# Four layer norms: inverse square root by a power on Pool with one Newton step, for a bit seed with three

## The chip, the cores and the metric

The kernel runs on one NeuronCore of one Trainium2 chip. The metric is the device time of one execution in microseconds (us): the median over several executions. A core has five engines that run their own instruction streams in order: PE (TensorE, matrix products; PEld is its weight load), DVE (VectorE), ACT (ScalarE), POOL (GpSimd) and SP (SyncE, which only issues transfers here). They wait for each other through semaphores, and an engine that waits holds everything queued behind.

## The reference

The input is x of 16 sequences (b) by 256 tokens by 128 features, float32. Two transformer-like layers follow, each a sum of a residual and a block on a layer norm:

```python
def _layernorm(x, axis=-1, eps=1e-05):
    m = jnp.mean(x, axis=axis, keepdims=True)
    v = jnp.var(x, axis=axis, keepdims=True)
    return (x - m) / jnp.sqrt(v + eps)

x = x + softmax_attention(_layernorm(x), ...)     # 16 heads of 8, scores 256 x 256
x = x + recurrence(_layernorm(x), ...)            # state over the 16 sequences: c = f*c + i*g; h = tanh(x wo + c uo + bo)
x = x + linear_attention(_layernorm(x), ...)      # rope, elu + 1 features, kv = sum k v, out / denom
x = x + mixture_of_experts(_layernorm(x), ...)    # 16 experts, the best 2 of each token, gelu between two products
```

So four norms are taken of every token. One norm needs 1/sqrt(v + eps) for each token. Tokens lie on the 128 partitions, two tiles of 128 tokens to a sequence (`TT = 2`), so the inverse roots of a sequence and a norm are a 128x2 array: very little data, and a chain of dependent steps.

## The kernel before

The program has three stages, each a block in which every engine runs its own loop over n, and each engine's instructions are written out by hand in a fixed order. Sequence b is at a different point of the pipeline in each part: "lag k" below is work on sequence n-k in iteration n.

**Stage 1** (`attention_and_recurrence`, n from -2 to 20) has softmax attention and the recurrence. PE does scores twice (once in p_max for the row maxima, which DVE reduces in `row_max`, L396, and once in p_exp, which ACT exponentiates, L551). Norm 1 of sequence n+2 and norm 2 of sequence n-3 run in iteration n. For each, DVE takes mean and variance in `layer_stats` (bn_stats, bn_aggr into `mv`), then three small instructions make the seed: v = var + eps (L382), the bits of v shifted right by one (L384), and 0x5F3759DF minus that (L387). Pool then does `newton_steps` (L67 to L74, four instructions a step, three steps) on the 128x2 array, and `layer_norm` (L315, L317: subtract the mean, multiply by the root). Behind each norm of sequence n+2 Pool has `setup` (once) and the split of q and k into bfloat16 parts (L337, L340, L342), which SP writes to a scratch array in DRAM and reads back as QS and KS before PE can start the scores.

**Stage 2** (`linear_attention_and_routing`, n from 0 to 20) has the h of the recurrence, linear attention, norms 3 and 4, and the routing to experts. Norm 3 of sequence n and norm 4 of sequence n-3 share one 128x4 array `root[r]`. Before the change DVE does the whole root in `root_step`, 13 instructions (L1012, L1015, L1019, then three times L1027, L1029, L1031, then L1035, which makes -mean*root), put one by one between DVE's other instructions. Signals `sd` and `nw` count them. ACT waits for `nw` before xn3 of sequence n-1 (L1267) in iteration n, and before `pay`, norm 4 of n-4 (L1302). ACT runs in this order in an iteration: xn3 (lag 1), hT = tanh(zs) (lag 0, L1273), on3T, xn3T, the exp and relu of rot, pay (lag 4), and more. PE, also in order, turns on3 (lag 3), xn3 (lag 1) and hT (lag 0; all L1349), then does p_u (L1376) and p_qkv (L1385, L1387). DVE adds p_h and p_u into X (L1078, L1085), casts the places of the tokens of sequence n-5 into `pos` (L1090), takes the statistics, makes rope products t (L1138 to L1149), KVm (L1167), the routing (among them z, L1202, and wheref, L1213), and ends with zs of the next iteration (L1054).

Pool in stage 2 has, per iteration: four indirect DMAs that scatter the rows of sequence n-5 into `disp` (L969, they wait for `pos`), an update of the row numbers (L976), the residual add of sequence n-4 (L983), and rot of sequence n-1, the sum of two rope products (L990).

**Stage 3** (`experts`) runs 80 tiles of 128 tokens through their experts, gathers and adds; the change doesn't touch it.

`steady` is an empty instruction that stops two instructions from being joined.

Of the kernel before, what the change touches and what calls it, by code (L numbers as in the profile page):

```python
# [13 lines left out]
P = 128  # L14
# [16 lines left out]
MAGIC = 0x5F3759DF  # L31
NEWTON = 3
# [27 lines left out]
def newton_steps(t, pool, root, mark, b):  # L60

    y, u, v = root[:, 0, :], root[:, 1, :], root[:, 3, :]
    j = 0
    for _ in range(NEWTON):
        if j:
            pool.wait_ge(mark.sem, mark.at(b, j))
        pool.tensor_tensor(u, y, y, ALU.mult).then_inc(mark.sem, 1)  # L67
        pool.wait_ge(mark.sem, mark.at(b, j + 1))
        pool.tensor_tensor(u, u, v, ALU.mult).then_inc(mark.sem, 1)
        pool.wait_ge(mark.sem, mark.at(b, j + 2))  # L70
        steady(pool, t)
        pool.tensor_scalar(u, u, -0.5, 1.5, ALU.mult, ALU.add).then_inc(mark.sem, 1)
        pool.wait_ge(mark.sem, mark.at(b, j + 3))
        pool.tensor_tensor(y, y, u, ALU.mult).then_inc(mark.sem, 1)  # L74
        j += 4


def constants(pool, t, w):

    n = 0  # L80
    fills = [(t["ident"], 0.0), (t["ident16"], 0.0), (w["kv_mask"], 1.0), (w["before"], 1.0),
# [29 lines left out]
def attention_and_recurrence(nc, ctx, t, out_dbg=None):  # L111
# [8 lines left out]
    with ExitStack() as scope:  # L120
# [57 lines left out]
        seed_a = sig("seed_a", 3)  # L178
        newton_a = sig("newton_a", 4 * NEWTON)
# [29 lines left out]
        seed_b = sig("seed_b", 3)  # L209
        newton_b = sig("newton_b", 4 * NEWTON)  # L210
# [87 lines left out]
        def _(pool):  # L298
# [20 lines left out]
            newton = lambda root, mark, b: newton_steps(t, pool, root, mark, b)  # L319

            def iteration(n, r):
                if active(n, -2):
                    pool.wait_ge(seed_a.sem, seed_a.at(n + 2))
                    q = (r + 2) % RING
                    newton(root1[q], newton_a, n + 2)
                    if xnT_p.due(n + 2 - RING):
                        pool.wait_ge(xnT_p.sem, xnT_p.at(n + 2 - RING))
                    layer_norm(n + 2, mv1[q], root1[q], xn1[q], newton_a, norm_a)
# [23 lines left out]
                if active(n, 3):  # L352
                    b, q = n - 3, (r - 3) % RING
                    pool.wait_ge(seed_b.sem, seed_b.at(b))
                    newton(root2[q], newton_b, b)
                    if xn2T_p.due(b - RING):
                        pool.wait_ge(xn2T_p.sem, xn2T_p.at(b - RING))
                    layer_norm(b, mv2[q], root2[q], xn2[q], newton_b, norm_b)
# [4 lines left out]
        def _(dve):  # L363
# [7 lines left out]
            def layer_stats(b, stats, mv, root, st, sd, prev_norm):  # L371
# [5 lines left out]
                for i in range(TT):  # L377
# [3 lines left out]
                dve.wait_ge(st.sem, st.at(b))  # L381
                dve.tensor_scalar(root[:, 3, :], mv[:, :, 1], EPS, None, ALU.add).then_inc(sd.sem, 1)  # L382
                dve.wait_ge(sd.sem, sd.at(b, 1))
                dve.tensor_scalar(root[:, 4, :].bitcast(U32), root[:, 3, :].bitcast(U32), 1, None, ALU.logical_shift_right)\  # L384
                    .then_inc(sd.sem, 1)
                dve.wait_ge(sd.sem, sd.at(b, 2))
                dve.tensor_scalar(root[:, 0, :].bitcast(I32), root[:, 4, :].bitcast(I32), -1.0, float(MAGIC), ALU.mult, ALU.add)\  # L387
                    .then_inc(sd.sem, 1)
# [50 lines left out]
            def iteration(n, r):  # L439
# [8 lines left out]
                for s in range(8):  # L448
# [26 lines left out]
                    if s == 5 and active(n, 3):  # L475
                        b, q = n - 3, (r - 3) % RING
                        dve.wait_ge(x1_s.sem, x1_s.at(b))
                        layer_stats(b, stats2[q], mv2[q], root2[q], stats_b, seed_b, norm_b)
# [4 lines left out]
                    if s == 1 and active(n, -2):  # L483
                        q = (r + 2) % RING
                        layer_stats(n + 2, stats1[q], mv1[q], root1[q], stats_a, seed_a, norm_a)
# [279 lines left out]
def linear_attention_and_routing(nc, ctx, t):  # L765
# [5 lines left out]
    with ExitStack() as scope:  # L771
# [46 lines left out]
        st3, sd, nw, nm3 = sig("st3", 4), sig("sd", 3), sig("nw", 3 * NEWTON + 1), sig("nm3", 2)  # L818
# [109 lines left out]
        def _(pool):  # L928
# [25 lines left out]
            def iteration(n, r):  # L954
# [23 lines left out]
                if active(n, 4):  # L978
# [5 lines left out]
                        .then_inc(res.sem, 1)  # L984
                if active(n, 1):
# [9 lines left out]
        def _(dve):  # L995
            def root_step(m, r, step):

                if not (active(m, 0) or active(m, 3)):
                    return
                y, u, shift, v = (root[r][:, j, :] for j in range(4))  # L1000
                newton = step - 3
                if step == 0:

                    if active(m, 0):
                        dve.wait_ge(st3.sem, st3.at(m))
                    if active(m, 3):
                        dve.wait_ge(st4.sem, st4.at(m - 3))
                    if active(m, PAIR):
                        dve.wait_ge(nm3.sem, nm3.at(m - PAIR))
                    if nm4.due(m - 3 - PAIR):  # L1010
                        dve.wait_ge(nm4.sem, nm4.at(m - 3 - PAIR))
                    dve.tensor_scalar(v, mv[r][:, :, 1], EPS, None, ALU.add).then_inc(sd.sem, 1)  # L1012
                elif step == 1:
                    dve.wait_ge(sd.sem, sd.at(m, 1))
                    dve.tensor_scalar(u.bitcast(U32), v.bitcast(U32), 1, None, ALU.logical_shift_right).then_inc(sd.sem, 1)  # L1015
                elif step == 2:

                    dve.wait_ge(sd.sem, sd.at(m, 2))
                    dve.tensor_scalar(y.bitcast(I32), u.bitcast(I32), -1.0, float(MAGIC), ALU.mult, ALU.add).then_inc(sd.sem, 1)  # L1019
# [724 lines left out]
```

## Time and profile before

| what | us |
|---|---|
| median of 3 runs | 832.79 (830.95 to 838.27) |
| the profiled execution, its own time | 830.77 |
| its span in the profile | 828.8 |
| busy: PE / DVE / POOL / ACT | 607.7 / 508.8 / 365.4 / 343.1 |
| stage 1, stage 2, stage 3 (about) | 0 to 405, 405 to 641, 641 to 829 |
| mean granted TensorE clock | 0.88 of full speed |

The time of the profiled execution is 2.0 us more than the span, which goes from the first to the last instruction. Busy times are sums of one engine's instructions and say nothing about who waits for whom; the rows further down do. The stages meet at barriers, so a time saved within a stage moves everything behind it.

### The profile page before, as it was taken

To read this page: it belongs to the slowest core of one execution; us is meant where nothing else is said; L and a number is where in the kernel's file an instruction comes from. 1 tells how busy PE (TensorE), PEld (TensorE's weight loads), DVE (VectorE), ACT (ScalarE), POOL (GpSimd) and SP (SyncE) were. 2 spreads that over 40 slices of the span, in tenths; PEclk is the share of its full clock that TensorE was granted. 3 is DMA by queue.
4 is the path that set the end of the run, shared out by engine and by line. 5 is a ranking of instruction groups with operands and counts; after the bars stand their busy time and mean duration, and the time that the engine had idled before them with its cause. 6 is when DMAs were issued, how large, how long until landed. Compare 5 with 4: busy or idle time off the path is not lost. (4 is left out here: it accounts for less than half of the span.)

```text
span 828.8 us, 17046 instructions
## 1 busy us (share of the span) xinstructions
PE 607.7 (73%) x4308; PEld 412.5 (50%) x4309; DVE 508.8 (61%) x1745; ACT 343.1 (41%) x725; POOL 365.4 (44%) x747
## 2 busy tenths in 40 slices
PE   1378899999999999997457667667662388788850
PEld 0134555555555555554235455445442277677740
DVE  6277877777777777753177887888765122222214
ACT  1015666666666666663224444444431122222210
POOL 5533555555555553222311345455446055555553
PEclk9999999999999999998666787787655599999995
DMA  5333332222222222100430000000001322222108
GB/s 139 95 109 96 99 98 82 79 73 76 79 72 73 77 78 76 34 2 1 80 129 2 16 24 27 13 26 23 20 23 50 78 76 72 72 71 74 53 15 302
DMA packets 49537, 55.62 MB, mean 67 GB/s; under 512 B 11229, under 2 KB 42658, under 8 KB 46914
## 3 DMA queue, kind: packets, MB, share of 16 engines
q1 hardware_dynamic: 43714, 45.87, 19.5%
q0 software_dynamic: 4608, 8.47, 3.1%
q8 instruction: 28, 0.46, 0.2%
q10 hardware_dynamic: 1152, 0.53, 0.2%
q14 instruction: 35, 0.29, 0.1%
HBM read 36.44 MB, written 19.02 MB: 67 GB/s over the span
## 5 line engine op out<-in xcount | busy, mean ns | idle before, releaser
L396 DVE TENSOR_REDUCE negmax<-p_max 128x2 f32<-128x512 f32 x256 | 172.6, 687 | 63.9 <-PE p_max L605 63.0
L551 ACT ACTIVATE probs<-p_exp 128x1024 f32<-128x1024 f32 x128 | 129.3, 1025 | 9.4 <-PE p_exp L580 9.4
L1536 POOL DMA_INDIRECT back<-y,rows x80 | 78.3, 979 | 84.1 <-DVE y L1597 61.0
L605 PE MATMUL p_max<-KS,QS 96*128 96x256 bf16 x512 | 102.4, 286 | 9.3 <-DMA QS<-scratch 6.9
L969 POOL DMA_INDIRECT disp<-pay,pos x64 | 63.0, 984 | 94.9 <-ACT pay L1302 49.7
L67 POOL TENSOR_TENSOR root<-root 128x2 f32<-128x2 f32 x96 | 18.6, 193 | 170.1 <-DVE root L387 165.0
L595 PE MATMUL p_out<-probs,V 128*32 128x256 f32 x1024 | 81.8, 391 | 1.3 <-ACT OT L567 0.7
L580 PE MATMUL p_exp<-QS,KS 128*128 128x256 bf16 x512 | 78.0, 275 | 2.5 <-DMA QS<-maxT 2.5
L1597 DVE TENSOR_TENSOR y<-p_y,rows 128x256 f32<-128x256 f32 x40 | 16.9, 424 | 100.1 <-PE p_y L1661 88.2
L605 PEld LDWEIGHTS p_max<-KS,QS 96*128 96x128 bf16 x512 | 43.6, 100 | 55.2 <-DVE negmax L396 25.5
L1648 PE MATMUL p_hid<-xT,w 128*128 128x128 f32 x320 | 59.5, 307 | 0.0
L580 PEld LDWEIGHTS p_exp<-QS,KS 128*128 128x128 bf16 x512 | 48.1, 98 | 18.0 <-issue 7.8
L1616 ACT ACTIVATE hid<-p_hid 128x512 f32<-128x512 f32 x40 | 23.9, 598 | 75.7 <-remote 49.2
L1661 PE MATMUL p_y<-W,hid 128*128 x320 | 51.0, 294 | 0.0
L1648 PEld LDWEIGHTS p_hid<-xT,w 128*128 128x128 f32 x320 | 49.8, 196 | 1.5
L1646 PE MATMUL p_hid<-ones,bp 128*128 128x128 bf16 x160 | 35.8, 224 | 14.6 <-issue 13.5
L1661 PEld LDWEIGHTS p_y<-W,hid 128*128 128x128 f32 x320 | 41.8, 190 | 1.9
L1611 ACT ACTIVATE xT<-p_x 128x256 f32<-128x256 f32 x40 | 15.3, 381 | 49.3 <-PE p_x L1634 46.9
L1590 DVE COPY w<-W 128x256 f32 x80 | 22.7, 303 | 19.0 <-issue 19.0
L595 PEld LDWEIGHTS p_out<-probs,V 128*32 128x32 f32 x1024 | 20.2, 108 | 27.5 <-issue 19.9
L1439 PE MATMUL p_r<-sel,before 128*128 128x16 bf16 x16 | 3.1, 191 | 40.7 <-DVE sel L1242 40.7
L990 POOL TENSOR_TENSOR rot<-t 128x512 f32<-128x512 f32 x16 | 20.2, 1262 | 27.8 <-DVE t L1149 27.8
(229 smaller groups left out, 1367.6 us busy)
## 6 DMA issues: line engine op xcount, KB each, us to landing
KS<-scratch SPq DMA_DIRECT2D x16, 576.0 KB
QS<-scratch SPq DMA_DIRECT2D x48, 192.0 KB
scratch<-part SPq DMA_DIRECT2D x16, 384.0 KB, 2.7
rows<-disp SPq DMA_DIRECT2D x80, 65.0 KB
yb<-back SPq DMA_DIRECT2D x8, 512.0 KB, 6.5
W<-in_W_dram SPq DMA_DIRECT2D x1, 2064.0 KB, 8.8
W<-in_W_dram SPq DMA_DIRECT2D x1, 2048.0 KB, 13.1
out_dram<-X SPq DMA_DIRECT2D x8, 256.0 KB, 5.9
```

Of the source, the lines that this page charges most:

```text
L396: dve.tensor_reduce(negmax[:, i, 2 * hp:2 * hp + 2], p_max[u % 2][:, :].rearrange("p (h k) -> p h k", h=2), AX.X, ALU.max, negate=True).th ...
L551: act.activation(probs[s % 2][:, :, :].rearrange("p j q -> p (j q)"), p_exp[s % 2][:, :], ACT.Exp)\
L580: mm = pe.matmul(p_exp[s % 2][:, j * S:(j + 1) * S], KS[q][:, h, kt * P:(kt + 1) * P], QS[q][:, h, :], start=True, stop=True)
L595: mm = pe.matmul(p_out[32 * j:32 * j + 32, 0:S], V[q][:, kt, 4 * g + j, :], probs[s % 2][:, j, :], start=(kt == 0), stop=(kt == 1))
L605: mm = pe.matmul(p_max[u % 2][:, j * S:(j + 1) * S], QS[q][0:PADDED, h, i * P:(i + 1) * P], KS[q][0:PADDED, h, :], start=True, stop=True)
L969: pool.indirect_dma_start(out=disp, out_offset=bass.IndirectOffsetOnAxis(ap=pos[o][:, i, k:k + 1], axis=0), in_=pay[o][:, k, i, :], in_off ...
L1536: pool.indirect_dma_start(out=back, out_offset=bass.IndirectOffsetOnAxis(ap=rows[r][:, h, D + 1:ROW].bitcast(U32), axis=0), in_=y[r][:, h, :],
L1590: dve.tensor_copy(w1[r][:, h, :], w["W1"][:, bass.ds(es[h], 1), 0:HID].rearrange("p o c -> p (o c)")).then_inc(w_s.sem, 1)
L1616: act.activation(hid[q][:, :, :, :].rearrange("p h c t -> p (h c t)"), p_hid[q % 2][:, :], ACT.Gelu).then_inc(hid_s.sem, 1)
L1646: pe.matmul(dst, w["bp"][:, bass.ds(es[h], 1), c * P:(c + 1) * P].rearrange("p o c -> p (o c)"), w["ones16"][:, :], start=True, stop=False)
L1648: mm = pe.matmul(dst, w1[q][:, h, c * P:(c + 1) * P], xT[q][:, h * P:(h + 1) * P], start=False, stop=True)
L1661: mm = pe.matmul(dst, hid[q][:, h, c, :], w["W2"][:, bass.ds(es[h], 1), c, :].rearrange("p o c -> p (o c)"), start=False, stop=(c == 1))
```

## The change

Pool's newton_steps becomes `inverse_root`: v = var + eps, then y = v to the power -0.5 as a tensor_tensor operation with an array `power` that holds -0.5, then one Newton step of four instructions. The seed instructions leave DVE in stage 1. In stage 2 all of `root_step` leaves DVE; Pool does inverse_root on the 128x4 array and two more instructions for -mean*root, eight in all, between the residual add (L983) and rot (L990). `nw` now counts eight, and DVE's and ACT's waits for `nw` stay where they were. One memset, of `power`, is added to `constants`.

```diff
-MAGIC = 0x5F3759DF
-NEWTON = 3
+ROOT_STEPS = 6
...
-def newton_steps(t, pool, root, mark, b):
+def inverse_root(t, pool, var, root, mark, b):
     y, u, v = root[:, 0, :], root[:, 1, :], root[:, 3, :]
...
+    steady(pool, t)
+    pool.tensor_scalar(v, var, EPS, None, ALU.add).then_inc(mark.sem, 1)
+    pool.wait_ge(mark.sem, mark.at(b, 1))
+    pool.tensor_tensor(y, v, t["power"][:, 0:v.shape[1]], ALU.pow).then_inc(mark.sem, 1)
+    pool.wait_ge(mark.sem, mark.at(b, 2))
+    pool.tensor_tensor(u, y, y, ALU.mult).then_inc(mark.sem, 1)
+    pool.wait_ge(mark.sem, mark.at(b, 3))
+    pool.tensor_tensor(u, u, v, ALU.mult).then_inc(mark.sem, 1)
+    pool.wait_ge(mark.sem, mark.at(b, 4))
+    steady(pool, t)
+    pool.tensor_scalar(u, u, -0.5, 1.5, ALU.mult, ALU.add).then_inc(mark.sem, 1)
+    pool.wait_ge(mark.sem, mark.at(b, 5))
+    pool.tensor_tensor(y, y, u, ALU.mult).then_inc(mark.sem, 1)
...
# stage 1, Pool, norm 1 (norm 2 alike)
-                    pool.wait_ge(seed_a.sem, seed_a.at(n + 2))
+                    pool.wait_ge(stats_a.sem, stats_a.at(n + 2))
-                    newton(root1[q], newton_a, n + 2)
+                    inverse_root(t, pool, mv1[q][:, :, 1], root1[q], root_a, n + 2)
...
# stage 1, DVE, layer_stats
-                dve.tensor_scalar(root[:, 3, :], mv[:, :, 1], EPS, None, ALU.add).then_inc(sd.sem, 1)
-                dve.tensor_scalar(root[:, 4, :].bitcast(U32), root[:, 3, :].bitcast(U32), 1, None, ALU.logical_shift_right)\
-                dve.tensor_scalar(root[:, 0, :].bitcast(I32), root[:, 4, :].bitcast(I32), -1.0, float(MAGIC), ALU.mult, ALU.add)\
...
# stage 2, Pool, between the residual add and rot; root_step and its 13 calls leave DVE
+                if active(n, 0) or active(n, 3):
+                    if active(n, 0):
+                        pool.wait_ge(st3.sem, st3.at(n))
+                    if active(n, 3):
+                        pool.wait_ge(st4.sem, st4.at(n - 3))
...
+                    inverse_root(t, pool, mv[r][:, :, 1], root[r], nw, n)
+                    pool.wait_ge(nw.sem, nw.at(n, ROOT_STEPS))
+                    pool.tensor_tensor(root[r][:, 2, :], mv[r][:, :, 0], root[r][:, 0, :], ALU.mult).then_inc(nw.sem, 1)
+                    pool.wait_ge(nw.sem, nw.at(n, ROOT_STEPS + 1))
+                    steady(pool, t)
+                    pool.tensor_scalar(root[r][:, 2, :], root[r][:, 2, :], -1.0, None, ALU.mult).then_inc(nw.sem, 1)
```

Where the instructions stand in the program can be seen at two places.

On Pool in stage 2, in an iteration of the steady part (here the first behind the hardware loop), before:

```order
L969 DMA disp<-pay,pos 67712x130 x4
L976 TENSOR_SCALAR pay<-pay 128x4
L983 TENSOR_TENSOR X<-X,pay 128x256
L990 TENSOR_TENSOR rot<-t 128x512
L969 DMA disp<-pay,pos 67712x130 x4
```

and the same iteration now:

```order
L956 DMA disp<-pay,pos 67712x130 x4
L963 TENSOR_SCALAR pay<-pay 128x4
L970 TENSOR_TENSOR X<-X,pay 128x256
L63 TENSOR_SCALAR root<-mv 128x4
L65 TENSOR_TENSOR root<-root,power 128x4
L67 TENSOR_TENSOR root<-root 128x4
L69 TENSOR_TENSOR root<-root 128x4
L72 TENSOR_SCALAR root<-root 128x4
L74 TENSOR_TENSOR root<-root 128x4
L986 TENSOR_TENSOR root<-mv,root 128x4
L989 TENSOR_SCALAR root<-root 128x4
L995 TENSOR_TENSOR rot<-t 128x512
```

The eight root instructions stand behind the four DMAs and the residual add, and rot behind them.

On DVE in stage 2, from the last statistics of an iteration on, before:

```order
L1116 BN_AGGR mv<-stats_1 128x2 x2
L1012 TENSOR_SCALAR root<-mv 128x4
L1126 SCALAR_TENSOR_TENSOR feat<-ex,rl 128x512
L1015 TENSOR_SCALAR root<-root 128x4
L1019 TENSOR_SCALAR root<-root 128x4
L1027 TENSOR_TENSOR root<-root 128x4
L1138 TENSOR_TENSOR t<-p_qkv,cosf 128x512
L1029 SCALAR_TENSOR_TENSOR root<-root 128x4
L1143 TENSOR_TENSOR t<-p_qkv,sinf 128x64x4
L1031 SCALAR_TENSOR_TENSOR root<-root 128x4
L1149 TENSOR_TENSOR t<-p_qkv,sinf 128x64x4
L1027 TENSOR_TENSOR root<-root 128x4
```

and now:

```order
L1098 TENSOR_TENSOR t<-p_qkv,cosf 128x512
L1102 TENSOR_TENSOR t<-p_qkv,sinf 128x64x4
L1107 TENSOR_TENSOR t<-p_qkv,sinf 128x64x4
L1115 TENSOR_REDUCE negtop<-p_r 128x2
L1123 TENSOR_TENSOR KVm<-p_kvo,kv_mask 128x144
```

The 13 root instructions are gone, and the others keep their order.

## Rows read from the trace of the kernel before

**Rows 1.** The page: span, and busy time of each engine.

```profile
span 828.8 us, 17046 instructions
PE 607.7 (73%) x4308; PEld 412.5 (50%) x4309; DVE 508.8 (61%) x1745; ACT 343.1 (41%) x725; POOL 365.4 (44%) x747
```

**Rows 2.** Who waited for whom, 100 to 400 us: total, times, longest.

```profile
POOL root L67 <- DVE root L387: 122.6, 25, 13.9
PE p_misc L693 <- DVE maxpart L411: 11.6, 13, 1.3
```

**Rows 3.** Timeline of POOL, the first 25 us: start, duration, instruction.

```profile
10.38 0.19 POOL L67 TENSOR_TENSOR root<-root 128x2 f32<-128x2 f32 x1 [6.32 <-DVE root L387]
10.65 0.20 POOL L69 TENSOR_TENSOR root<-root 128x2 f32<-128x2 f32 x1
11.01 0.19 POOL L72 TENSOR_SCALAR root<-root 128x2 f32<-128x2 f32 x1 [0.17 <-POOL root L69]
...
13.97 0.61 POOL L315 TENSOR_TENSOR xn<-X,mv 128x256 f32<-128x256 f32 x1
...
17.89 0.19 POOL L67 TENSOR_TENSOR root<-root 128x2 f32<-128x2 f32 x1
...
22.87 1.15 POOL L337 TENSOR_TENSOR rest<-qk,part 128x512 f32<-128x512 f32 x1
```

**Rows 4.** Timeline of DVE, and then of PE, in the same start of stage 1.

```profile
9.24 0.37 DVE L380 BATCH_NORM_AGGREGATE mv<-stats 128x2 f32<-128x6 f32 x2
...
38.68 1.04 PE L605 MATMUL p_max<-KS,QS 96*128 96x256 bf16 x4 [6.92 <-DMA QS<-scratch]
```

**Rows 5.** Timeline of DVE in stage 2, one steady iteration from pos to pos.

```profile
536.14 0.16 DVE L1090 CAST pos<-posf 128x4 uint32<-128x4 f32 x1
...
537.27 0.25 DVE L1116 BATCH_NORM_AGGREGATE mv<-stats 128x2 f32<-128x6 f32 x2
...
540.94 0.31 DVE L1167 TENSOR_TENSOR KVm<-p_kvo,kv_mask 128x144 f32<-128x144 f32 x1 [0.26 <-PE p_kvo L1413]
...
543.37 1.21 DVE L1213 CAST wheref<-where 128x4 f32<-128x4 uint32 x1
...
545.59 0.42 DVE L1054 TENSOR_TENSOR zs<-p_h,UC 128x256 f32<-128x256 f32 x1
...
548.56 0.16 DVE L1090 CAST pos<-posf 128x4 uint32<-128x4 f32 x1
```

**Rows 6.** Timeline of POOL in the same iteration.

```profile
537.43 1.06 POOL L969 DMA_INDIRECT disp<-pay,pos  x1 [5.93 <-ACT pay L1302]
...
542.65 0.68 POOL L983 TENSOR_TENSOR X<-X,pay 128x256 f32 x1
543.29 1.26 POOL L990 TENSOR_TENSOR rot<-t 128x512 f32<-128x512 f32 x1
```

**Rows 7.** Timeline of DVE: pos of iterations 6 and 15.

```profile
473.40 0.16 DVE L1090 CAST pos<-posf 128x4 uint32<-128x4 f32 x1
...
585.94 0.16 DVE L1090 CAST pos<-posf 128x4 uint32<-128x4 f32 x1
```

**Rows 8.** From xn3 to PE's turn of hT: ACT and PE timelines, iteration 2.

```profile
426.31 0.88 ACT L1267 ACTIVATE xn<-X,root 128x128 f32<-128x128 f32 x2 [1.91 <-DVE root L1035]
...
427.73 0.63 PE L1349 MATMUL p_h<-ident,hT 128*128 128x128 f32 x2
```

**Rows 9.** Chain of work that ended last: PE's turn of hT, iteration of rows 5.

```profile
546.78 0.43 PE p_h L1349 x2
```

**Rows 10.** Timeline of DVE: X gets p_h in iterations 1 and 2, before any scatter.

```profile
419.87 0.42 DVE L1078 TENSOR_TENSOR X<-p_h,X 128x256 f32<-128x256 f32 x1 [1.78 <-PE p_h L1349]
...
428.40 0.42 DVE L1078 TENSOR_TENSOR X<-p_h,X 128x256 f32<-128x256 f32 x1 [1.78 <-PE p_h L1349]
```

**Rows 11.** End of stage 2, iteration 18: residual add on POOL, and pay on ACT.

```profile
627.54 0.68 POOL L983 TENSOR_TENSOR X<-X,pay 128x256 f32<-128x256 f32 x1
...
628.67 1.09 ACT L1302 ACTIVATE pay<-X,root 128x256 f32<-128x256 f32 x2 [3.68 <-issue]
```

More of the change, by code:

```diff
@@ L57, in steady @@
     eng.nop(nofuse=True)
-def newton_steps(t, pool, root, mark, b):
+def inverse_root(t, pool, var, root, mark, b):
     y, u, v = root[:, 0, :], root[:, 1, :], root[:, 3, :]
[L63 to L75, printed above, removed]
+    steady(pool, t)
[11 more added lines that the diff above has]
+    pool.tensor_tensor(y, y, u, ALU.mult).then_inc(mark.sem, 1)
 def constants(pool, t, w):
     n = 0
-    fills = [(t["ident"], 0.0), (t["ident16"], 0.0), (w["kv_mask"], 1.0), (w["before"], 1.0),
+    fills = [(t["power"], -0.5), (t["ident"], 0.0), (t["ident16"], 0.0), (w["kv_mask"], 1.0), (w["before"], 1.0),
              (w["ones16"], 1.0), (w["one_row"], 1.0)]
@@ L369, in _, with layer_stats @@
             dve.wait_ge(t["v_set"].sem, 6)
-            def layer_stats(b, stats, mv, root, st, sd, prev_norm):
+            def layer_stats(b, stats, mv, st, prev_norm):
                 steady(dve, t)
@@ L984, in iteration @@
                         .then_inc(res.sem, 1)
+                if active(n, 0) or active(n, 3):
[3 more added lines that the diff above has]
+                        pool.wait_ge(st4.sem, st4.at(n - 3))
+                    if at(n, 0):
+                        pool.wait_ge(mv_set.sem, PAIR)
+                    if active(n, PAIR):
+                        pool.wait_ge(nm3.sem, nm3.at(n - PAIR))
+                    if nm4.due(n - 3 - PAIR):
+                        pool.wait_ge(nm4.sem, nm4.at(n - 3 - PAIR))
+                    inverse_root(t, pool, mv[r][:, :, 1], root[r], nw, n)
[4 more added lines that the diff above has]
+                    pool.tensor_scalar(root[r][:, 2, :], root[r][:, 2, :], -1.0, None, ALU.mult).then_inc(nw.sem, 1)
                 if active(n, 1):
@@ L995, in _ @@
         def _(dve):
[L996 to L1019, printed above, removed]
-                elif newton < 3 * NEWTON:
-                    if newton:
-                        dve.wait_ge(nw.sem, nw.at(m, newton))
-                    else:
-                        dve.wait_ge(sd.sem, sd.at(m))
-                    if newton % 3 == 0:
-                        dve.tensor_tensor(u, y, y, ALU.mult).then_inc(nw.sem, 1)
-                    elif newton % 3 == 1:
-                        dve.scalar_tensor_tensor(out=u, in0=u, scalar=-0.5, in1=v, op0=ALU.mult, op1=ALU.mult).then_inc(nw.sem, 1)
-                    else:
-                        dve.scalar_tensor_tensor(out=y, in0=u, scalar=1.5, in1=y, op0=ALU.add, op1=ALU.mult).then_inc(nw.sem, 1)
-                else:
-                    dve.wait_ge(nw.sem, nw.at(m, 3 * NEWTON))
-                    dve.scalar_tensor_tensor(out=shift, in0=mv[r][:, :, 0], scalar=-1.0, in1=y, op0=ALU.mult, op1=ALU.mult).then_inc(nw.sem, 1)
             def wide(ap, shape):
@@ L1678, in program @@
         t["back"] = nc.dram_tensor("back", [TOP * TOKENS, D], F32).ap()
-        t["count"] = sb("count", [P, E])
+        t["count"], t["power"] = sb("count", [P, E]), sb("power", [P, 2 * TT])
         w = t["w2"] = dict(wo=sb("wo", [P, D]), uo=sb("uo", [P, D]), bo=sb("bo2", [P, 1]), Wqkv2=sb("Wqkv2", [P, 3 * D]),
```

39 lines of the change are left out of this document (9 added, 30 removed).

## The prediction

> **What bounds the kernel now.** I read the page's engine line first, then the table of waits of stage 1, then the timelines of Pool, DVE, ACT and PE where a root is made. The page shows PE and DVE ahead of Pool in busy time [rows 1], which seems to say that work should go from DVE to Pool. The other views say where this is so.
>
> In the steady part of stage 1 it isn't worth anything. Pool stood idle for 122.6 us in 300 before it got a seed, 25 times [rows 2], so its norms are nowhere late, and PE runs through; its largest wait for DVE is 11.6 us in all for the split of the maxima [rows 2], which starts behind the last row maximum and not behind a seed. Only the start of stage 1 hangs on roots: Pool is the path there. It starts the first root at 10.38, the first norm at 13.97, the second root at 17.89, and can split q and k of the first sequence only at 22.87 [rows 3]; PE's first scores at 38.68 wait for the transfers that follow from it [rows 4].
>
> In stage 2 the busy DVE is not the engine that sets the pace. Follow one iteration from pos to pos, 536.14 to 548.56, 12.42 us [rows 5]. The cast gives pos; Pool's four scatters start at 537.43, the residual add at 542.65, rot at 543.29, and rot ends at 544.55 [rows 6]. DVE's cast of 4 columns to wheref starts at 543.37 and takes 1.21 us, so it ends when rot does [rows 5]. From its end DVE runs through to zs and to the next pos in 4.0 us. So the loop goes through Pool: pos, scatters, add, rot, wheref, pos. Over nine iterations the mean is (585.94 - 473.40)/9 = 12.50 us [rows 7]. KVm in the middle waits for PE [rows 5], so DVE's first half wouldn't be much earlier without root instructions either.
>
> The Trainium skill (SBUF — State Buffer, section "SBUF: two separate sides") says that an operation of GpSimd and one of VectorE with two SBUF inputs or in a two-port mode lock each other out for a whole instruction. The wheref row agrees. By that rule each of eight new Pool instructions could hold a DVE instruction of this kind once; at 0.2 us each this would be 1.6 us of DVE's time an iteration, against the 1.2 us that the wait of wheref gives back.
>
> **The power.** No row shows one. I call its excess e the time that it takes beyond the 0.19 us of a multiply of the same shape [rows 3]. From below it is zero, as it can't be done faster than a multiply. From above the nearest row is a scatter, in which Pool works through 128 descriptors in 1.06 us [rows 6]: e up to 0.9. I take e = 0.3 for 128x4 and half of that for 128x2, nearer to the multiply, since 4 columns are little for 128 lanes; this is a guess between the two, and the largest open cost. A dearer power is a rival below.
>
> **Part by part.** Steps of a chain on Pool start 0.27 us apart, and 0.36 us where `steady` stands between [rows 3].
>
> Start of stage 1. The statistics end at 9.61 [rows 4]; the first norm may start at 9.66 + 0.27 (v) + 0.27 (power) + 0.27 + 0.36 + 0.27 + 0.34 = 11.44 + e/2, for 13.97 now [rows 3]: -2.5 (0.7 of it are DVE's three seed instructions). The second root has six instructions for twelve: 1.85 for 3.7, another -1.9. Together -4.4 + e = **-4.1 us**; it all comes through, as Pool is without a gap from there to the split, but for a set-up that moves along. The added memset is one of 0.2 us at the head, beside six us of idle Pool ahead of the first root: nothing.
>
> Steady part and end of stage 1: **0**. Covered by the idle Pool time; if the cover were gone, the 2 x 6 instructions fewer would be a gain of 3 us an iteration, so it is no risk either. DVE's six seed instructions, under 1.4 us an iteration (twice the 0.7 above), stand beside a PE that doesn't wait for them.
>
> Stage 2, first iterations. There are no scatters yet, and a root on Pool starts right behind the statistics. Its chain is eight steps: 0.28 + 0.28 + 0.28 + 0.37 + 0.28 + 0.28 + 0.37 and 0.23 for the last = 2.4 to 2.5 + e (a hundredth each for 4 columns in place of 2). From X to X iterations 1 and 2 are 8.53 us apart [rows 10]. Now: X to the end of statistics 1.36 (pos to the end of statistics is 1.38 in rows 5, and here X stands in the place of pos), 0.06, root 2.45 + e, then from the start of xn3 to PE's turn of hT 1.42 [rows 8] and 0.67 to X [rows 8, 10]: 6.0 + e, a gain of 2.5 - e. The next three intervals have more DVE work of their own, and gain what 13 small instructions (0.16 us for the cast of 4 columns, [rows 5], so 2.1 together) leave beside waits for PE: bounds are 0 and 2.1 each, and I take 1.1, 1.1 and 0.5, the last with less since Pool's add comes in. In iteration 0 Pool may still be busy with the split of the biases (see the program); I estimate the root there late by 0.3 + e, for which no row is shown. Sum: -4.9 + 2e = **-4.3 us**.
>
> Stage 2, steady. In front of xn3 (ACT), and so in front of hT behind it, and PE's turn of xn3 and hT, now stands Pool's root, which stands behind four scatters. From rows 5, 6: pos to first scatter 1.29, first scatter to the end of the add 5.86, root 2.45 + e, xn3 to the turn of hT 1.42 [rows 8], the turn of hT at 546.78 [rows 9] to the next pos at 548.56, 1.78. Sum 12.80 + e, against 12.50 now: +0.3 + e. Rot is later by 2.45 + e too, but the wait for it by wheref is gone, since wheref now comes ahead of rot; DVE by itself would need about 11.4 us (12.5 less the 1.0 by which wheref is longer than a cast of 4 columns, 0.16, [rows 5]), which is covered by the new path. Eleven intervals, from iteration 5 to 16, hold a norm 3 in this place: 11 x 0.6 = **+6.6 us**. With e from 0 to 0.9 and the first term from -0.3 to +0.5 (the 1.29 is 1.0 in other iterations, where the new path has less to fill): 0 to +15.
>
> Stage 2, end. The root of iteration 18 was ready early. Now it follows the add, which ends at about 628.2 [rows 11], and takes to 630.7 + e; pay, which started at 628.67 [rows 11], can start only then: +2.1 + e; the last scatters and the plan of the tiles follow from it, and a few tenths from the wait of iteration 16's pay. **+2.7 us**.
>
> Sum: -4.1 - 4.3 + 6.6 + 2.7 = +0.9, so the profiled execution's 830.8 becomes 831.7. The median of the three runs is 2.0 above that execution, so I forecast 833 as a median.
>
> **Rivals.**
> Slow power: if Pool evaluates it element after element, e is above 1. It decides from e = 0.8 on (e stands in the sum 1 + 2 + 11 + 1 = 15 times, so each 0.1 costs 1.5 us). At e = 2 the sum is -4.4 - 4.9 + 3.3 + 2.4 + 15 x 2 = +26, 859 us. For it: nothing else on Pool in the trace is a transcendental, and its other work is cheap only because it is a multiply or an add. Against: one remaining Newton step fits a fast, rough evaluation. This is the case on the slower side.
>
> DVE is the bound after all: Pool's root comes early enough, or the clock of PE rises as the pace does, and each steady interval loses the wait of wheref or the 13 instructions, about 1.1 us. Then -4.1 - 4.3 - 12 + 2.7 = -18, 815 us. For it: DVE is busy in most of stage 2. Against: the order on Pool puts the root behind 7.2 us of other work.
>
> The first power waits for code: a routine is loaded when Pool meets the instruction first, in the start of stage 1, on the path. The trace shows no such gap for Pool's first instruction of other kinds [rows 3]. By bounds between nothing and the 4.1 us that this part gains, the sum would be up to 4 higher, 837.
> The Trainium skill (GPSIMD Engine Reference, section "Instruction dispatch") says about 6 us for the first call of a freshly loaded kernel; the sum would be 839 by it. No row shows one.
>
> The change may also not do what it says in one way: if the compiler turned the power into several instructions; that is the slow power again.
>
> **How the numbers follow.** 1% (8 us) is about what a measurement of this kernel can tell from no change. Forecast (e up to 0.8): 0.57, 825 to 841. Slow power: 0.24, 841 to 870 or more. DVE bound: 0.15, 812 to 824. Code load: 0.04, near 838. Faster by over 1%: 0.15 and 0.03 of the forecast's low edge = 0.18. Slower by over 1%: 0.24 and 0.11 of its high edge and of the code load = 0.35. The rest, 0.47, is within 1%. The range from 820 to 858 leaves out a tenth at either side.
>
> **What the profile after would show.** The power's row on Pool gives e. The first norm at about 11.6 for 13.97, PE's first scores at about 34.6. In stage 2 wheref at 0.2 us instead of 1.2, ACT's xn3 waiting for Pool's last root instruction, hT right behind xn3, pos to pos near 13.1. If pos to pos falls below 12, the Pool path isn't what I take it for; if it is over 14, the power is slow or Pool's small instructions are held by DVE.

## The result, and the profile after

The changed kernel takes 840.88 us (median, 837.61 to 844.65), the kernel before 832.22 us (829.03 to 838.27) on the same chip: a ratio of 1.009, 95% interval 1.007 to 1.011 (the quotient of the two medians is 1.010, within that interval). It is 0.9% slower, where I had forecast +0.1%.

The page of the changed kernel, with the group of the new instruction (columns as in [rows 1]; in the group: instructions, busy time and mean ns of one, idle time before them):

```profile
span 837.3 us, 16537 instructions
...
PE 607.3 (73%) x4308; PEld 413.0 (49%) x4309; DVE 449.9 (54%) x1402; ACT 341.9 (41%) x725; POOL 395.6 (47%) x708
...
L65 POOL TENSOR_TENSOR root<-root,power 128x2 f32<-128x2 f32 (+1 forms) x51 | 42.8, 839 | 4.2
```

DVE lost 58.9 us of busy time [rows 1], Pool gained 30.2, and the span grew by 8.5. The power alone is 42.8 us of Pool's time.

The start of stage 1, Pool and then PE:

```profile
9.77 0.24 POOL L63 TENSOR_SCALAR root<-mv 128x2 f32<-128x2 f32 x1 [5.66 <-DVE mv L375]
10.10 0.72 POOL L65 TENSOR_TENSOR root<-root,power 128x2 f32<-128x2 f32 x1
...
12.14 0.61 POOL L312 TENSOR_TENSOR xn<-X,mv 128x256 f32<-128x256 f32 x1
...
16.17 0.22 POOL L63 TENSOR_SCALAR root<-mv 128x2 f32<-128x2 f32 x1
...
19.77 1.16 POOL L332 TENSOR_TENSOR rest<-qk,part 128x512 f32<-128x512 f32 x1
...
35.14 1.03 PE L592 MATMUL p_max<-KS,QS 96*128 96x256 bf16 x4 [6.49 <-DMA QS<-scratch]
```

The first norm starts at 12.14 for 13.97 [rows 3], the split at 19.77 for 22.87, PE's first scores at 35.14 for 38.68 [rows 4]: -3.5 us. The very first power takes 0.72 us, as the later ones of two columns do, so no load shows in it.

One steady iteration of stage 2, from pos to pos, on DVE:

```profile
531.56 0.16 DVE L1054 CAST pos<-posf 128x4 uint32<-128x4 f32 x1
...
536.45 0.31 DVE L1123 TENSOR_TENSOR KVm<-p_kvo,kv_mask 128x144 f32<-128x144 f32 x1 [0.49 <-issue]
...
538.21 0.61 DVE L1164 CAST wheref<-where 128x4 f32<-128x4 uint32 x1
...
539.82 0.42 DVE L1018 TENSOR_TENSOR zs<-p_h,UC 128x256 f32<-128x256 f32 x1
...
540.72 0.22 DVE L1038 TENSOR_REDUCE posf<-mine 128x4 f32<-128x64 f32 x1
544.44 0.42 DVE L1042 TENSOR_TENSOR X<-p_h,X 128x256 f32 x1 [3.49 <-PE p_h L1300]
...
545.63 0.16 DVE L1054 CAST pos<-posf 128x4 uint32<-128x4 f32 x1
```

and on Pool:

```profile
532.84 1.10 POOL L956 DMA_INDIRECT disp<-pay,pos  x1 [3.93 <-ACT pay L1253]
...
538.11 0.68 POOL L970 TENSOR_TENSOR X<-X,pay 128x256 f32 x1
538.88 0.22 POOL L63 TENSOR_SCALAR root<-mv 128x4 f32<-128x4 f32 x1
539.18 1.04 POOL L65 TENSOR_TENSOR root<-root,power 128x4 f32<-128x4 f32 x1
...
541.85 0.24 POOL L989 TENSOR_SCALAR root<-root 128x4 f32<-128x4 f32 x1 [0.16 <-POOL root L986]
542.05 1.26 POOL L995 TENSOR_TENSOR rot<-t 128x512 f32<-128x512 f32 x1
```

and what waits for the root on ACT, then PE's turn of hT:

```profile
542.23 0.49 ACT L1218 ACTIVATE xn<-X,root 128x128 f32 x1 [4.98 <-POOL root L989]
...
543.64 0.63 PE L1300 MATMUL p_h<-ident,hT 128*128 128x128 f32 x2
```

DVE is done with everything it has at 540.94, and then stands idle for 3.49 us. It waits for PE. There p_h waits for hT, hT stands behind xn3 in ACT's order, and xn3 waits 4.98 us for Pool's last root instruction. The root itself starts when the four scatters and the residual add are issued, though its input, mv, is ready at 532.94. That is the path of the prediction. It is 14.07 us long, by its five pieces: pos to first scatter 1.28, first scatter to root 6.04, root to xn3 3.35, xn3 to the turn of hT 1.41, on to pos 1.99. The two pos that answer to [rows 7]:

```profile
460.86 0.16 DVE L1054 CAST pos<-posf 128x4 uint32<-128x4 f32 x1
...
587.51 0.16 DVE L1054 CAST pos<-posf 128x4 uint32<-128x4 f32 x1
```

(587.51 - 460.86)/9 = 14.07 us, for 12.50. At the end of the stage pay waits 6.63 us for the last root, where it had waited for no root before [rows 11], and starts at 636.23, for 628.67:

```profile
636.23 1.09 ACT L1253 ACTIVATE pay<-X,root 128x256 f32<-128x256 f32 x2 [6.63 <-POOL root L989]
```

Set side by side at the same events, the 8.5 us of the span are: first scores -3.5; on to the first X of stage 2 another -4.6; from there to the pos of iteration 5 -4.6; iterations 5 to 16 +15.4; 16 to 20 +4.7; from there to the first transpose of stage 3 -0.7; stage 3 +1.7.

### The profile page after: what moved, and what is told of

Read it like the earlier page. It is cut to its first block, busy times and chain, and to the rows that moved or that the text cites. A ratio compares the mean times of both kernels' runs of the same rounds, so it can differ in the third digit from the quotient of the medians.

```text
span 837.3 us, 16537 instructions
## 1 busy us (share of the span) xinstructions
PE 607.3 (73%) x4308; PEld 413.0 (49%) x4309; DVE 449.9 (54%) x1402; ACT 341.9 (41%) x725; POOL 395.6 (47%) x708
## 4 chain that ended last, share of the span: by engine, by line
PE 19%; POOL 11%; issue 10%; ACT 4%; DVE 3%; DMA 2%; SPq 1%; POOLq 1%; another core or an unknown queue 0%; ACTq 0%; DVEq 0%
PE p_hid L1599 5%; PE p_y L1612 5%; POOL disp L956 5%; POOL root L65 2%; PE p_hid L1597 2%; PE p_ta L1300 1%; ACT pay L1253 1%; PE p_x L1585 1%; POOL X L970 1%; PE p_y L1609 1%; ACT xn L1218 1%; DMA yb<-back 1%; ACT rl L1243 1%; PE p_u L1327 1%; DVE X L1476 1%
## 5 line engine op out<-in xcount | busy, mean ns | idle before, releaser
L63 POOL TENSOR_SCALAR root<-mv 128x2 f32<-128x2 f32 (+1 forms) x51 | 12.2, 240 | 207.4 <-DVE mv L375 195.5
L567 PEld LDWEIGHTS p_exp<-QS,KS 128*128 128x128 bf16 x512 | 48.3, 98 | 19.4 <-issue 7.8
L65 POOL TENSOR_TENSOR root<-root,power 128x2 f32<-128x2 f32 (+1 forms) x51 | 42.8, 839 | 4.2
L1612 PEld LDWEIGHTS p_y<-W,hid 128*128 128x128 f32 x320 | 41.9, 190 | 2.5 <-issue 0.5
L1218 ACT ACTIVATE xn<-X,root 128x128 f32<-128x128 f32 (+1 forms) x32 | 14.0, 485 | 61.8 <-POOL root L989 61.8
L1300 PE MATMUL p_ta<-ident,xn 128*128 128x128 f32 x32 | 10.6, 432 | 33.1 <-ACT xn L1218 33.1
```

What stands on the lines that cost most here:

```text
L65: pool.tensor_tensor(y, v, t["power"][:, 0:v.shape[1]], ALU.pow).then_inc(mark.sem, 1)
L567: mm = pe.matmul(p_exp[s % 2][:, j * S:(j + 1) * S], KS[q][:, h, kt * P:(kt + 1) * P], QS[q][:, h, :], start=True, stop=True)
L1612: mm = pe.matmul(dst, hid[q][:, h, c, :], w["W2"][:, bass.ds(es[h], 1), c, :].rearrange("p o c -> p (o c)"), start=False, stop=(c == 1))
```

## The experiments

Chips differ (the kernel before took 833.7, 837.5 and 822.1 us beside the three groups of four runs), so ratios to it are compared, and intervals inside a trace. "Interval" is (pos of iteration 16 less pos of iteration 5)/11: 12.53 us before, 13.94 after. The first and the last of these eleven can be short or long by themselves, so where it matters the mean of the nine between iterations 6 and 15 is given too: 12.50 before, 14.07 after.

**The change in one stage only.** First stage 1 alone:

```diff
 # stage 1
-newton(root1[q], newton_a, n + 2)
+inverse_root(t, pool, mv1[q][:, :, 1], root1[q], root_a, n + 2)
 # stage 2: root_step on DVE as before
```

> The change in stage 1 alone; stage 2 keeps its 13 root instructions on DVE. By the two traces stage 1 of the changed kernel ends 8.1 us earlier (last state 404.34 and 396.24), in three places: the start, the last two iterations, and 0.17 us in each steady iteration. If these belong to the change, this kernel takes 832.2 - 8.1 = 824 us, a ratio of 0.990. If only the start does, as I forecast, and the rest is chance between two executions, it is 832.2 - 3.5 = 828.7, 0.996.

825.2 us, ratio 0.991 (0.987 to 0.995). Then stage 2 alone, with the bit seed left in stage 1:

> The change in stage 2 alone; stage 1 keeps the bit seed and three Newton steps. By the traces stage 2 loses 15.4 us from iteration 5 to 16 and about 5 at its end, and gains 4.5 in its first iterations: 832.2 + 16.7 = 849 us, ratio 1.020. The sum of the prediction with the measured power (e = 0.85) gives +12.7 + 3.2 - 3.2 = +12.7, 845, ratio 1.015. A rival by which DVE was the bound and stage 2 gained has it at or under 832.

850.1 us, ratio 1.019 (1.015 to 1.023), interval 14.06. So the change is two changes of opposite sign: about -8 us in stage 1 and +16 in stage 2. Both runs came out where the two traces had put them; of the two forecasts for stage 1 alone, the one by which only the start gains (0.996) lies outside the measured interval.

**The power as a multiply.** The same instructions, with a cheap one in the power's place (the roots are then not roots):

```diff
-    pool.tensor_tensor(y, v, power, ALU.pow)
+    pool.tensor_tensor(y, v, power, ALU.mult)     # power filled with 0.3
```

> The changed kernel with a multiply in the place of the power on Pool (by 0.3, so that the roots are wrong, and with them what follows), all else the same. It takes 0.84 us less on 128x4 and 0.53 less on 128x2. If the root lies on the path where I think, it is 11 x 0.84 in the steady part of stage 2, 3 x 0.84 at its ends and 2 x 0.53 at the start, with two more of 0.53 at the end of stage 1: 840.9 - 13.9 = 827 us, 0.994 of the kernel before. If Pool is not the path in stage 2, only the ends gain: 837 us or more.

830.3 us, ratio 0.995 (0.992 to 0.997), as expected. The interval is 13.29 us: of the 1.41 us by which it grew, 0.65 go with the power's excess (I had expected all of its 0.84), and 0.76 would be there with a power as cheap as a multiply.

**The root ahead of the scatters.** Pool's order in stage 2: root, scatters, row numbers, residual add, rot.

```diff
+                # root of iteration n, first on Pool
                 if active(n, 5):
                     # four scatters
                 ...
-                # root of iteration n
                 # rot
```

> The changed kernel with Pool's eight root instructions of stage 2 ahead of the four scatters in place of behind the residual add; the same instructions. The root starts at the statistics (1.4 us after pos) and xn3 waits no more; scatters, add and rot come 3.3 us later, rot at about 11 us after pos, which holds exp, relu and pay of the next iteration. I estimate 12.0 to 12.4 us from pos to pos in place of 14.0: 840.9 - 18 to 22 - 3 (end of stage 2) = 817 to 820 us, ratio 0.983. If the loss comes from the amount of work on Pool or from its hold on DVE, not from the place of the root, it stays at 838 or above.

837.95 us, ratio 1.006 (1.003 to 1.008): only 3 us of the 20 that I expected, and the very time that I had given the rival, more work on Pool. The interval is 13.51 us (14.13 between iterations 6 and 15), short and long ones in turn: 9.2, 18.3, 10.0, 18.5 and so on. Pool, DVE and ACT of this kernel, around a pos:

```profile
543.44 1.26 POOL L995 TENSOR_TENSOR rot<-t 128x512 f32<-128x512 f32 x1
543.75 0.98 DVE L1054 CAST pos<-posf 128x4 uint32<-128x4 f32 x1
...
544.73 0.63 ACT L1242 ACTIVATE ex<-rot 128x512 f32<-128x512 f32 x1 [3.15 <-POOL rot L995]
...
545.27 0.61 ACT L1243 ACTIVATE rl<-rot 128x512 f32<-128x512 f32 x1
...
545.79 1.08 ACT L1253 ACTIVATE pay<-X,root 128x256 f32 x2
```

The root no longer waits; rot does. It is now last on Pool, and ACT's order is ex, rl, pay, so pay, on which the router depends, waits for rot too, though it doesn't use it. Whether that is the cause, or the amount of work on Pool, the next run has to tell.

**Root and rot ahead of the scatters.**

> The changed kernel, with Pool's order in stage 2 turned to root, rot, then scatters, row numbers, residual add. With the root alone ahead (the run before this one) every second interval was long: rot stood last, ACT's ex, rl and with them pay waited for it. Theory, rot's place held that version back: pay no longer waits 3 us for rot, the interval from pos to pos falls from 14.1 to some 12.2 us, and the time is 820 us, ratio 0.985. Rival, Pool itself is full (root 3.3, rot 1.3, scatters 5, add 1.3, together 10.9 us, and what DVE locks out): the interval stays over 13 us and the time is 833 or more.

828.07 us, ratio 0.990 (0.985 to 0.996), interval (588.55 - 450.82)/11 = 12.52, between the theory and the rival. The work on Pool is the same as in the changed kernel, so the loss there came from its order: the places of root and rot together are worth 1.4 us an iteration, or 1.0 by the nine inner ones (13.03 for 14.07). By these this kernel is still 0.5 slower an iteration than the one before, and it gains only what it gets ahead of the first scatters: 41.1 us from the first X to the pos of iteration 5, for 46.4. I had expected 12.2. ACT's pay now waits for the scatters, whose buffer it fills:

```profile
528.12 1.09 ACT L1253 ACTIVATE pay<-X,root 128x256 f32 x2 [2.12 <-DMA disp<-pay,pos]
```

The trace shows another wait too, which the scatters and the add on Pool bring with them. Pool's residual add, and DVE's add of p_u just ahead of pos:

```profile
526.72 0.68 POOL L994 TENSOR_TENSOR X<-X,pay 128x256 f32 x1
...
527.50 0.42 DVE L1049 TENSOR_TENSOR X<-p_u,X 128x256 f32 x1 [1.92 <-PE p_u L1327]
```

Nothing in the program makes DVE's add wait for Pool's. Yet in the six iterations from 488 to 554 us it starts 0 to 0.15 us after Pool's ends. Pool has no gap to speak of from the root on: from pos at 514.97 to the root 1.6 us, then root, rot, scatters and add up to 527.40, then pos at 527.84. So in this order Pool's own work is the loop, which is what the rival said, if at a smaller price.

**Only rot ahead, the root still last.** The fourth corner of the square:

> The changed kernel with only rot moved ahead of the scatters, the root still last. Theory, the path is pos, statistics, t, rot, scatters, add, root, xn3, hT, pos: rot starts some 4 us behind pos in place of a scatter at 1.3, everything behind it is later by about 4 us, interval 18 us, time 880 or more. Rival, moving rot forward is what helped the other version, and the root's place matters little: 14 us or less an interval, 838 or less.

884.89 us, ratio 1.075 (1.071 to 1.079), interval 17.76. Pool in one iteration:

```profile
547.52 0.24 POOL L995 TENSOR_SCALAR root<-root 128x4 f32<-128x4 f32 x1 [0.16 <-POOL root L992]
554.84 1.26 POOL L948 TENSOR_TENSOR rot<-t 128x512 f32<-128x512 f32 x1 [7.07 <-DVE t L1107]
```

Pool stands idle for 7.07 us, because its first instruction waits for t, and the scatters, for which pos is there at 551.30, stand behind it. Of the four orders, ratios 1.009 (both last), 1.006 (root first), 1.075 (rot first), 0.990 (both first), only the last is faster than the kernel before. It is no faster than the change in stage 1 alone (0.991), so no order shows a gain from the root's move to Pool in stage 2.

**The power in the good order.** Root and rot first, and the power a multiply as above:

> The changed kernel with root and rot ahead of the scatters (0.990), and the power replaced by a multiply by a constant, so that the roots are not roots and the routing differs. Theory, in this order the root is off the path in the steady part: interval 12.4 to 12.5 us as with the power, and only the start and the first iterations gain, 3 to 5 us, ratio 0.985. Rival, the power still stands on the path: 11 times 0.85 more, ratio 0.974.

802.42 us, ratio 0.976 (0.972 to 0.979), interval (579.81 - 449.31)/11 = 11.86. I expected no change of interval; it fell by 0.66 us (by 1.1 between iterations 6 and 15, from 13.03 to 11.91), and the ratio fell by 0.014, as in the late order. So the rival holds: the root is not off the path there, since rot, the scatters and the add stand behind it on Pool.

**What set the pace before.** The prediction read the loop as pos, scatters, add, rot, wheref. Here stage 1 is changed, stage 2 has its old root on DVE, and rot goes ahead of the scatters:

> Change in stage 1 only; stage 2 with the bit seed on DVE as before, but rot ahead of the scatters on Pool. Theory (the prediction's reading of the kernel before: pos, scatters, add, rot, wheref held by rot, pos): wheref takes 0.2 us in place of 1.2, the interval falls from 12.5 to about 11.6 us, and the time is 816 us, 9 under the 825.2 of the same kernel with the old order. Rival, another chain of the same length stands behind it (ACT's and PE's through pay and the router): 825, and wheref is short all the same.

825.44 us, ratio 0.987 (0.982 to 0.992). wheref is short at last:

```profile
522.07 0.21 DVE L1220 CAST wheref<-where 128x4 f32<-128x4 uint32 x1
```

but the interval is only (588.29 - 453.57)/11 = 12.25, for 12.49 in the same kernel with rot last (12.32 for 12.50 between iterations 6 and 15), and the 95% intervals of the two ratios, 0.987 and 0.991, overlap. A wait of 1 us was taken away, and some 0.2 came of it. The trace shows where the rest went. From pos to zs the nine inner iterations take 8.74 us, for 9.44 with rot last; but from DVE's add of p_h to its add of p_u they take 1.40, for 0.92. With rot first, the scatters and the residual add come later on Pool, and the add now falls in front of the add of p_u:

```profile
538.34 0.68 POOL L996 TENSOR_TENSOR X<-X,pay 128x256 f32 x1
...
539.11 0.42 DVE L1092 TENSOR_TENSOR X<-p_u,X 128x256 f32 x1 [1.12 <-PE p_u L1383]
```

The wait is put down to PE, but p_u is done at 537.63. In most steady iterations DVE starts within 0.3 us of the end of Pool's add. So a wait of DVE beside rot was exchanged for one beside the residual add. ACT's pay waits for the scatters' transfers here too (0.7 to 1.2 us); whether that costs anything isn't shown.

**Is it DVE?** The kernel before, with one Newton step in place of three in stage 2's root (two refinements are left out, six DVE instructions an iteration):

> The kernel before with one Newton step in place of three in stage 2's root on DVE: six small DVE instructions fewer an iteration, nothing moved (this leaves out two refinement steps of the root). Theory, DVE doesn't set the pace of the steady part: interval still 12.3 to 12.5 us, only the first iterations gain, 829 us, ratio 0.996. Rival, DVE is the bound: six times 0.16 to 0.2 us an iteration off, interval 11.4 us, 815 to 818 us, ratio 0.98.

826.69 us, ratio 0.989 (0.984 to 0.995). The pos of iterations 5 and 16:

```profile
453.34 0.16 DVE L1090 CAST pos<-posf 128x4 uint32<-128x4 f32 x1
...
589.84 0.16 DVE L1090 CAST pos<-posf 128x4 uint32<-128x4 f32 x1
```

Interval 12.41, for 12.53: DVE doesn't set the steady pace. The gain lies ahead of it: from the first X to the pos of iteration 5 this kernel takes 39.5 us, the one before 46.4, the changed one 41.9. Without scatters the root on DVE stands on the path, and six instructions fewer are worth 6.9 us in five iterations. Whether by the shorter chain of the root or by DVE's time isn't separated. The kernel before loses time there in yet another way: in iterations 2 to 5 Pool's rot falls on a step of the root, which takes 1.26 us three times and 0.90 once, for 0.15 alone. Pool, and then DVE:

```profile
424.02 1.26 POOL L990 TENSOR_TENSOR rot<-t 128x512 f32<-128x512 f32 x1 [8.47 <-DVE t L1149]
...
424.04 1.26 DVE L1029 SCALAR_TENSOR_TENSOR root<-root 128x4 f32<-128x4 f32 x1
```

**Where stage 1's second half of the gain is from.** Stage 1 changed, and three seed instructions put back on DVE, for nobody:

```diff
+                dve.tensor_scalar(spare, mv[:, :, 1], EPS, None, ALU.add)
+                dve.tensor_scalar(spare.bitcast(U32), ..., 1, None, ALU.logical_shift_right)
+                dve.tensor_scalar(spare.bitcast(I32), ..., -1.0, float(MAGIC), ALU.mult, ALU.add)
```

> Change in stage 1 only (825.2 us measured), and three instructions of a bit seed put back on DVE behind each layer norm's statistics, into a row that nobody reads. The root on Pool doesn't wait for them. Theory, about 4 of the 8 us that stage 1 gained come from DVE being free sooner for its row maxima: 829 us, and the wait of PE for negmax is back near 15.7 us in 100 to 400 us. Rival, all of it comes from the shorter chain on Pool: 825 to 826 us.

827.24 us, ratio 0.989 (0.985 to 0.993). Its waits of 100 to 400 us, and then those of the changed kernel (total, times, longest):

```profile
PEld p_max L621 <- DVE negmax L412: 15.7, 36, 0.9
```

```profile
PEld p_max L592 <- DVE negmax L383: 12.0, 27, 0.9
```

The wait is back, as both theories allow, and costs nothing: from the first state to the fourteenth this kernel takes 260.3 us, the one with the change in stage 1 alone 260.1, the kernel before 261.9. The relief of DVE is not where the gain is from. By exclusion it is the chain on Pool, which is shorter and no longer waits for a seed; the path by which PE gets the 1.8 us isn't shown.

**What a power costs.** The kernel before, with powers and multiplies of six sizes put at the head of Pool:

> The kernel before with twelve extra instructions on Pool at its head, whose results nobody reads: power, then multiply, of 1, 2, 4, 8, 16 and 64 columns in 128 partitions. From 0.72 us for two columns and 1.04 for four: a fixed 0.4 and 0.16 a column, so 0.56, 0.72, 1.04, 1.7, 3.0 and 10.6 us, and multiply 0.19 up to 16 columns. Rival, the cost goes by steps of columns and flattens: 64 columns under 5 us.

It ran once, and only the instructions' times are read. The powers of 1 to 16 columns, and then of 16 and 64 (instructions, then ns of the shortest, the median and the longest):

```profile
L117 POOL TENSOR_TENSOR probe<-probe_in,probe_exp x5: 580/1007/2897, 4.5 to 8.3; 128x1 f32<-128x1 f32 x1, 128x2 f32<-128x2 f32 x1, 128x4 f32<-128x4 f32 x1, 128x8 f32<-128x8 f32 x1
...
L117 POOL TENSOR_TENSOR probe<-probe_in,probe_exp x2: 2897/6720/10543, 8.3 to 11.1; 128x16 f32<-128x16 f32 x1, 128x64 f32<-128x64 f32 x1
```

0.58 us for one column, 1.01 for four, 2.90 for 16, 10.54 for 64: (10.54 - 2.90)/48 = 0.159 us a column and 0.35 to 0.42 fixed, with no flattening.

**A version from the pieces.** Stage 1 as changed; in stage 2 rot ahead of the scatters, the roots of iterations 1 to 5 on Pool with the power, all others on DVE with the seed:

```diff
+        def pool_roots(n):
+            return isinstance(n, int) and 1 <= n <= 5
```

> A kernel put together from what the runs point to: stage 1 as changed; in stage 2 rot ahead of the scatters; the root of iterations 1 to 5, before any scatter, on Pool with the power, all later ones on DVE with the bit seed. Theory: the gain of the first iterations (4.6 us from the first X to the pos of iteration 5 in the changed kernel) adds to the kernel with rot first and the old root (0.987): ratio 0.981 to 0.983, some 4 to 5 us less. Rival, the iterations behind take it back, since the first scatters wait for something else: 0.987.

803.33 us, ratio 0.977 (0.974 to 0.979): faster than both kernels, and by a little more than expected. The first X to the pos of iteration 5 takes 41.8 us, as in the changed kernel, and the interval is (587.27 - 452.11)/11 = 12.29, as with the old root and rot first (but 12.61 for 12.32 between iterations 6 and 15). The profiled execution was the slowest of the five, 808.3 us, which is 0.983 of the kernel before and what I had expected; what the other four gained beyond it no trace shows.

## Why the prediction was right or wrong

The range held the time and the mechanism stood; the central value was 0.9% low (by the prediction's own sum, 831.7 + 2.0, it should have been 833.7 and not 833). That it was so near is in part luck. The power's cost was much too low, the steady iterations of stage 2 lost more than forecast beyond that, and most of this was made up by a gain in stage 1 that the sum put at nothing. With the measured cost of the power the sum would be +9.4 us for the 8.5 measured, but its parts miss by -0.2, -4.6, -1.4, +2.8, +1.4 and +1.0, in the order of the program.

- **The power.** e = 0.3 was the term that was most wrong: "since 4 columns are little for 128 lanes" was a guess. Four columns take 1.04 us for 0.19, so e = 0.85, and two take 0.53 more, not 0.15. This is the slow power of the rivals ("it decides from e = 0.8 on") at its very edge, not at e = 2. The rule there, 1.5 us for each 0.1 of e, makes 8 us of the 0.55 missed; that this is just about the whole miss is the luck said above. The run with the multiply bears the rule out: its ratio, 0.995 for 1.009, is some 12 us for e = 0.85, where the rule says 13.
- **Start of stage 1.** -4.1 forecast, -3.5 measured at the first scores. With 0.53 for a power of two columns in place of 0.15, twice, the sum would have been -4.4 + 1.1 = -3.3.
- **Steady part and end of stage 1.** 0 forecast, -4.6 measured; "covered by the idle Pool time" was not all. 1.8 us come in 13 intervals, from the first to the fourteenth state (260.1 to 260.5 us in ten traces with the new stage 1, 261.9 to 262.5 in four with the old), and not through DVE. 0.5 came before, from the first scores to the first state. The last two intervals brought 2.3 in the profiled run and belong to the clock of PE, not to the change: PE's busy time in them fell by the same 2.3 us (13.1 to 10.9). 1.6 of the 2.3 are in eight gate products near the end. Before, and then after, PE's busy time and granted clock in that stretch (length, busy time and instructions of PE, PEld, DVE, ACT, Pool, granted clock, DMA share, GB/s):

```profile
397.70:401.30 3.60, 3.53 (x8) 2.32 (x8) 0.00 (x0) 0.00 (x0) 0.00 (x0) 0.54 0.00 0
```

```profile
391.20:393.30 2.10, 1.97 (x8) 1.42 (x8) 0.00 (x0) 0.09 (x1) 0.00 (x0) 1.00 0.00 0
```

  These eight products ran at about half clock (1.2 GHz) before and at full clock (2.4 GHz) after, 1.6 us apart. In the other 12 traces the two intervals take 19.3 to 23.1 us (20.8 before, 18.5 after), and the nine with the new stage 1 among them 21.8 to 22.8: the 2.3 us were chance. Over all traces (without the one with the twelve extra instructions) the last state comes at 398.4 us on the mean with the new stage 1 and at 405.1 with the old, 6.7 us apart, of which 3.5 are there at the first scores. So the term that I put at nothing is about -3 and not -4.6.
- **Stage 2, first iterations.** -4.3 forecast, -4.6 measured, in spite of the dearer power: its formula, -4.9 + 2e, gives -3.2 with e = 0.85. The step from X to X of iterations 1 and 2 ([rows 10], 8.53 us) takes 419.31 - 412.45 = 6.86 us, a gain of 1.7 where 2.5 - e says 1.65. The next intervals gained 1.4, 2.1 and 0.4 where I took 1.1, 1.1 and 0.5. What I had overlooked is that rot holds a step of the root on DVE once in each of these iterations, 4.1 us together beyond the steps' own time, with xn3 waiting for the root [rows 8]; with the root on Pool, ahead of rot, this is gone. No run tests it by itself. But the old form itself takes 46.4 to 48.3 us here in five traces, the new one 41.1 to 42.5 in five, so the -4.6 of this pair could be 4 to 7.
- **Stage 2, steady.** +6.6 forecast, +15.4 measured. The path is the one described; the pieces were 1.29, 5.86, 2.45 + e, 1.42, 1.78 and measured 1.28, 6.04, 3.35, 1.41, 1.99. The root's piece holds 0.60 of the 0.97 missed (13.10 forecast, 14.07 measured), the two others that are longer 0.39. Of this 0.21 is a misreading: the turn of hT at 546.78 [rows 9] is not its start. The timeline has it at 546.57, so the last piece was 1.99 us in the kernel before too:

```profile
546.57 0.63 PE L1349 MATMUL p_h<-ident,hT 128*128 128x128 f32 x2
```

  The term's own range, 0 to +15, just missed the +15.4 (and its lower end, with -0.3 for the first term, is -3). The order on Pool, called there the reason against the DVE rival, is confirmed as the cause by the run that moves root and rot.
- **Stage 2, end.** +2.7 forecast; +4.7 measured to the pos of iteration 20. The last interval, in which pay waits for the root, takes 11.48 us for 8.67: +2.8, where 2.1 + e says 2.95. The other 1.9 come from the three intervals ahead of it (-1.7, +3.5 and +0.1); why isn't shown. Behind them stage 3 and the way to it took 1.0 us more, a term that the sum hasn't, and whether it belongs to the change isn't shown either.
- **The reading of the kernel before** (pos, scatters, add, rot, wheref) was right in its order and wrong in its weight: that chain could be cut by 1 us and the pace changed by 0.24. From wheref's end DVE does not run through to pos either, as the prediction has it: it waits 0.67 us for p_h and 0.43 for p_u. It cost the forecast nothing, as the new path is longer.
- **DVE is the bound**: fell, for the steady part, in the changed kernel itself, in which DVE stands idle, and in the run with one Newton step; for the five iterations ahead of the scatters the root on DVE is on the path. **Code load**: fell. The first power took 0.72 us. The Trainium skill (GPSIMD Engine Reference, section "Instruction dispatch") speaks of about 6 us for the first call to a freshly loaded kernel; no row here shows it.

Of the rest that I had named to look for: the first norm came at 12.14 for about 11.6, and PE's first scores at 35.14 for 34.6, both late by the dearer power; wheref took 0.15 to 0.21 us in nine of 13 iterations, and up to 0.64 in the others, as at 538.21 beside the residual add; xn3 waits for Pool's root; pos to pos was to be over 14 if "the power is slow or Pool's small instructions are held by DVE", and it was 14.07 with a slow power. Pool's small instructions weren't held: their steps are the same 0.27 and 0.36 us as in [rows 3].

## What to carry to other kernels

Work that is moved to an idle engine enters that engine's queue: before counting what it costs there, read what stands ahead of it and who waits behind it. Here stage 2's part of the change cost 16 us with the eight instructions behind four scatters. Ahead of them, and with the instruction that others waited for (rot) moved too, it cost nothing on balance: what the first iterations gained the steady ones took back. And where a cost is not in the trace, measure that one instruction first: one short run with six sizes would have taken the largest uncertainty out of this forecast.

## What the hardware did that I had not expected

- The time of a float power on Pool grows evenly with its columns: 0.159 us for each column of 128 partitions and some 0.4 fixed, from 1 to 64 columns, against 0.19 to 0.20 us for a whole multiply of two or four columns.
- A small cast on DVE of 0.16 us lasted to the end of a large operation that Pool ran beside it, and the wait wanders with the order: wheref beside rot (1.21 us, [rows 5]) in the kernel before, pos beside rot (0.98 us) with the root first, wheref beside the add (0.61 us) in the changed kernel. The Trainium skill (SBUF — State Buffer, section "SBUF: two separate sides") has GpSimd and a VectorE operation in a two-port mode or with two SBUF inputs lock each other out for a whole instruction, and these rows agree. Taking such a wait away is not the same as gaining it: with rot first, 1 us less at wheref was worth 0.24 us an iteration, since DVE then waited beside Pool's residual add.
- PE's granted clock is not the same at the same place of the program. Kernels with the same stage 1 differ by 4 us in its last two intervals (18.5 to 22.8), with granted clocks from 0.58 to 1.00 in them, which is as much as its root's change is worth at the first scores.
